# Softmax rows multiplied into W on GpSimd instead of VectorE, with one store per image

## Chip, cores and metric

One core of one Trainium2 chip. The metric is the device time of one execution in microseconds (us). The kernel before takes 877.63 us (median of 3 runs, 877.34 to 877.78).

## What is computed

For each of 32 images x of 384 channels and 1024 pixels (32 x 32), with 12 heads of 32 channels:

```python
w = einsum('bnc,oc->bno', group_norm(x), qkv_w)       # first product, split in 12 heads
w_normed = w / max(sqrt(sum over pixels of w*w), 1e-12)
Pi = softmax over heads of (sum over d of w_normed**2) * temp
Pi_n = Pi / (sum over pixels of Pi + 1e-8)
dots = einsum('bhn,bhnd->bhd', Pi_n, w * w)
attn = 1.0 / (1.0 + dots)
out = -(w * Pi) * attn                                # a row of Pi for each head, a number of attn for each channel
y = x + einsum('bnc,oc->bno', out, out_w) + out_b     # second product
```

All of it is in float32. Each product is computed as three TensorE products of rounded parts: high by high, low by high, high by low.

## The kernel before

Channels lie on the 128 partitions in T = 3 tiles of 128 channels by 1024 pixels (N). A tile of work on VectorE, ScalarE or GpSimd is thus 128x1024. The five engines each run a hand-written program whose order is fixed; semaphores alone tie them together. `pipeline` runs `step(i)` for i = 0 to 32: two steps written out, a loop over 28 images in fours, and the last ones written out. In step i the engines finish image i-2, carry out the second half of image i-1 and the first half of image i.

TensorE, step i: `first_product(i, t)` for t = 0, 1, 2 (W of image i into PSUM `acc`), then `second_product(i-1, t)` for t = 0, 1, 2. Inside the first of these, before its `UL` terms, stand the `head_sums(i)` (line 579), which need the sums of squares of all three tiles of image i, by way of VectorE's `head_sum_weights` (lines 717 to 731). The second product reads `UH` and `UL`, the high and low parts of W weighted by Pi and attn.

ScalarE, step i: `square_w(0)` (line 399, into WS, with the sum of squares), `keep_w(0)` (line 408, W from PSUM into WV), `u_hi(0)` (line 389, UH from WV), `square_w(1)`, `u_hi(1)`, `u_hi(2)`, `square_w(2)`, the two small group-norm activations, `keep_w(1)`, `keep_w(2)`, then `normalise` and `x_hi` for image i+1 (lines 416, 427), with the softmax exponentials between.

VectorE, step i: `finish(i-2, 2)` (line 849, product plus bias plus x, into X), `dot(i-1, t)` three times (line 769: Pi times squares, summed over pixels), the four small operations of `attention(i-1)` (lines 781 to 787), `weigh(i-1, t)` three times (line 795: WV times the scale times Pi, in place), `u_lo` for tiles 0 and 1 (line 841), `group_moments`, `head_sum_weights(i)`, `group_norm`, `u_lo` for tile 2, statistics of image i+2 (line 656), the softmax (lines 738 to 758, which ends with the rows PIT), more statistics, `finish(i-1, 0)` and `finish(i-1, 1)`.

GpSimd, step i: `x_lo(i+1, t)` three times (line 349: XL = XN - XH), nothing else.

SyncE, step i: store tile 2 of image i-2, wait for the stores of that image, load image i+2 (1.5 MB), `spread_pi(i)`: three small writes of PIT to HBM (line 309) and three reads (line 314) that bring the softmax rows back as PIB, spread over 32 partitions each and with 33 numbers for every 32 pixels; then store tiles 0 and 1 of image i-1.

The last image has an order of its own (`last_step`, `attend_last` at line 798): for each tile the dot, four small operations and the weighing (line 812) in turn, so that its UH can start early.

Of the kernel before, what the change touches and what calls it, by code (L numbers as in the profile page):

```python
# [27 lines left out]
ALU = mybir.AluOpType  # L28
ACT = mybir.ActivationFunctionType
# [17 lines left out]
IDLE_TURNS = (6, 3, 1, 15)  # L47
SM_SHIFTED, SM_STEPS = 3, 8
ATTENDED = 3 + 4
U_STEPS = ATTENDED + 3  # L50
LAST_ATTENDED, LAST_WEIGHED = 5, 6


class Image:
# [28 lines left out]
def conv_attention(nc, x, qkv_w, temp, out_w, out_b, y):  # L83
# [15 lines left out]
    with ExitStack() as ctx:  # L99
# [6 lines left out]
        def sem(name):  # L106
            return ctx.enter_context(nc.semaphore(name))
# [91 lines left out]
        pi_written = [sem(f"pi_written_{t}") for t in range(T)]  # L199
        pi_spread = [sem(f"pi_spread_{t}") for t in range(T)]  # L200
        u_step = sem("u_step")
        uh_done = sem("uh_done")
        ul_done = [sem(f"ul_done_{t}") for t in range(T)]
        m2_done = sem("m2_done")
# [14 lines left out]

            return not isinstance(j.number, int) or 0 <= j.number < B  # L220

        def weighed(j, t):

            if has(j) and not has(j + 1):
                return j.counts(U_STEPS, t * LAST_WEIGHED + LAST_WEIGHED)
            return j.counts(U_STEPS, ATTENDED + t + 1)

        def norm_of(j):

# [44 lines left out]
        @block.sync  # L274
        def _(sp):
            def load(j):
                if has(j):
                    if j.follows(2):
                        sp.wait_ge(x_loaded, j.counts(16, -16))
                    sp.dma_start(X[:, j.slot, :], j.of(x_img)).then_inc(x_loaded, 16)  # L280


            for t in range(T):
                sp.dma_start(x_tile(FIRST, t), FIRST.of(x_img)[:, t * N:(t + 1) * N]).then_inc(first_loaded[t], 16)
            sp.dma_start(raw_w1, qkv_w.rearrange("(t p) c -> p t c", t=T)).then_inc(w1_loaded, 16)
            sp.dma_start(raw_w2, out_w.rearrange("(p t) o -> p (t o)", t=T)).then_inc(w2_loaded, 16)
            for j in range(1, SLOTS):
                load(Image(j, j))

            def store(j, t):  # L290
                if has(j):
                    sp.wait_ge(y_done, j.counts(T, t + 1))
                    sp.dma_start(j.of(y_img)[:, t * N:(t + 1) * N], x_tile(j, t)).then_inc(y_stored, 16)

            def store_half(j, t, h):

                sp.wait_ge(y_done, j.counts(T, t + h + 1))
                columns = slice(t * N + h * BANK, t * N + (h + 1) * BANK)
                sp.dma_start(j.of(y_img)[:, columns], X[:, j.slot, columns]).then_inc(y_stored, 16)

            def spread_pi(j):

                if has(j):


                    sp.wait_ge(sm_step, j.counts(SM_STEPS, SM_STEPS))
                    for t in range(T):
                        rows = pi_dram[t * HPT:(t + 1) * HPT].rearrange("h (b q n) -> q (h b) n", b=BLOCKS, q=QUADS)
                        sp.dma_start(rows, PIT[:, t, :]).then_inc(pi_written[t], 16)
                    for t in range(T):  # L310
                        sp.wait_ge(pi_written[t], j.counts(16, 16))
                        heads = pi_dram[t * HPT:(t + 1) * HPT].unsqueeze(0)\
                            .to_broadcast([D, HPT, BLOCKS * QUADS * (QUAD + 1)])
                        sp.dma_start(PIB[:, t].rearrange("p b n -> p (b n)"), heads).then_inc(pi_spread[t], 16)

            def step(i):
                store(i - 2, 2)
                if has(i - 2) and has(i + 2):
                    sp.wait_ge(y_stored, (i - 2).counts(T * 16, T * 16))
                    load(i + 2)  # L320
                spread_pi(i)
                store(i - 1, 0)
                store(i - 1, 1)

            write_stats(sp, FIRST + 1)
            gather_stats(sp, FIRST + 1)
            pipeline(sp, step, 0, B)
            for h in range(HALVES):
                store_half(Image(B - 1, B - 1), T - 1, h)
            sp.wait_ge(y_stored, (B * T + HALVES - 1) * 16)  # L330

        @block.gpsimd
        def _(pool):

            pool.memset(identity[:], 0.0).then_inc(masks_step, 1)
            pool.memset(head_mask[:], 0.0).then_inc(masks_step, 1)
            pool.wait_ge(masks_step, 2)
            pool.affine_select(out=identity[:], in_=identity[:], compare_op=ALU.not_equal, fill=1.0, base=0,
                               pattern=[[-1, P]], channel_multiplier=1).then_inc(masks_step, 1)
            pool.wait_ge(w2_loaded, 16)  # L340
            pool.tensor_copy(mixed_w2.rearrange("p (m d h) -> p m d h", d=D, h=HPT),
                             raw_w2.rearrange("p (m h d) -> p m d h", d=D, h=HPT)).then_inc(w2_mixed, 1)

            def x_lo(j, t):
                if has(j) and j.follows(1):
                    pool.wait_ge(xn_done, j.counts(T, t + 1))
                    pool.wait_ge(xh_done, j.counts(T, t + 1))
                    pool.wait_ge(m1_done, j.counts(T))
                    pool.tensor_tensor(XL[:, t, :], XN[:, t, :], XH[:, t, :].bitcast(F32),  # L349
                                       ALU.subtract).then_inc(xl_done, 1)  # L350

            def step(i):
                for t in range(T):
                    x_lo(i + 1, t)

            pipeline(pool, step, 0, B)

        @block.scalar
        def _(act):
# [21 lines left out]
            def step(i):  # L381
                def u_hi(t):
                    j = i - 1
                    if has(j):
                        act.wait_ge(u_step, weighed(j, t))
                        if j.follows(1):
                            act.wait_ge(m2_done, j.counts(T))
                            act.wait_ge(ul_done[t], j.counts(1))
                        act.activation(UH[:, t, :], w_tile(j, t), ACT.Copy).then_inc(uh_done, 1)  # L389

                def square_w(t):
                    if has(i):
# [223 lines left out]
        def _(dve):  # L616
# [143 lines left out]
            def in_blocks(tile):  # L760
                return tile.rearrange("p (b n) -> p b n", n=QUAD)

            def dot(j, t):

                if has(j):
# [21 lines left out]
                    done = dve.scalar_tensor_tensor(dots[:, 3], total, SUM_FLOOR, inverse, ALU.add, ALU.mult)  # L787
                done.then_inc(u_step, 1)

            def weigh(j, t):  # L790

                if has(j):
                    dve.wait_ge(u_step, j.counts(U_STEPS, ATTENDED))
                    dve.wait_ge(w_kept, j.counts(T, t + 1))
                    dve.scalar_tensor_tensor(in_blocks(w_tile(j, t)), in_blocks(w_tile(j, t)), dots[:, 3, t:t + 1],  # L795
                                             PIB[:, t, :, 0:QUAD], ALU.mult, ALU.mult).then_inc(u_step, 1)

            def attend_last(j, t):

                total, dot_t, both, inverse = pi_tot[:, t:t + 1], dots[:, 0, t:t + 1], dots[:, 1, t:t + 1], dots[:, 2, t:t + 1]  # L800
                base = j.counts(U_STEPS, t * LAST_WEIGHED)
                dot(j, t)
                dve.tensor_reduce(total, PIB[:, t, :, QUAD], AX_X, ALU.add).then_inc(u_step, 1)
                dve.wait_ge(u_step, base + 2)
                dve.scalar_tensor_tensor(both, total, SUM_FLOOR, dot_t, ALU.add, ALU.add).then_inc(u_step, 1)
                dve.wait_ge(u_step, base + 3)
                dve.reciprocal(inverse, both).then_inc(u_step, 1)
                dve.wait_ge(u_step, base + 4)
                dve.scalar_tensor_tensor(dots[:, 3, t:t + 1], total, SUM_FLOOR, inverse, ALU.add, ALU.mult).then_inc(u_step, 1)
                dve.wait_ge(u_step, base + LAST_ATTENDED)  # L810
                dve.wait_ge(w_kept, j.counts(T, t + 1))
                dve.scalar_tensor_tensor(in_blocks(w_tile(j, t)), in_blocks(w_tile(j, t)), dots[:, 3, t:t + 1],  # L812
                                         PIB[:, t, :, 0:QUAD], ALU.mult, ALU.mult).then_inc(u_step, 1)

            def finish_half(j, t, h):

# [17 lines left out]
            def u_lo(j, t):  # L834

                if has(j):
                    dve.wait_ge(uh_done, j.counts(T, t + 1))
                    dve.wait_ge(u_step, weighed(j, t))
                    if j.follows(1):
                        dve.wait_ge(m2_done, j.counts(T))  # L840
                    dve.tensor_tensor(UL[:, t, :], w_tile(j, t), UH[:, t, :].bitcast(F32),  # L841
                                      ALU.subtract).then_inc(ul_done[t], 1)

            def finish(j, t):

# [6 lines left out]
            def step(i):  # L852
# [8 lines left out]
                weigh(i - 1, 0)  # L861
                weigh(i - 1, 1)
                weigh(i - 1, 2)
                u_lo(i - 1, 0)
                u_lo(i - 1, 1)
                group_moments(i + 1)
# [67 lines left out]
```

## Time and profile before

| | |
|---|---|
| median of 3 runs | 877.63 us |
| profiled execution | 877.32 us, span 875.4 us |
| TensorE (matmuls) busy | 855.1 us, 98% |
| VectorE busy | 746.8 us, 85% |
| ScalarE busy | 528.0 us, 60% |
| GpSimd busy | 225.5 us, 26% |
| mean share of the DMA engines, q1 | 51.9% |
| mean granted TensorE clock | 0.995 |

The span runs from the first to the last instruction of the profiled execution. Engines overlap, so the shares don't add up. The profile names PE for TensorE, PEld for its weight loads, DVE for VectorE, ACT for ScalarE, POOL for GpSimd, SP for SyncE; L769 is line 769. A busy share says how much an engine works, not which work the end waits for; that is in the chain of work that ended last.

### The profile page before, as it was taken

The numbers are of one execution on the slowest core, as the hardware profiler recorded it, in microseconds if no ns is written. First come the engines' busy times: TensorE is split into PE (matmuls) and PEld (weight loads), VectorE is DVE, ScalarE is ACT, GpSimd is POOL, SyncE is SP. The second block draws the span as 40 slices with busy tenths as digits, with TensorE's granted clock in tenths as the row PEclk, the third lists the DMA queues.
The fourth block names the chain that finished last, engine by engine and source line by source line (L and its number), as shares of the span: only waits on it lengthen the run. The fifth ranks groups of instructions, "written<-read, shape, count | busy, mean of one in ns | idle before, by whom it ended". The sixth has DMA issues, their size and how long they took to land.

```text
span 875.4 us, 14196 instructions
## 1 busy us (share of the span) xinstructions
PE 855.1 (98%) x4298; PEld 682.2 (78%) x4298; DVE 746.8 (85%) x1377; ACT 528.0 (60%) x676; POOL 225.5 (26%) x101
## 2 busy tenths in 40 slices
PE   6799999999999999999999999999999999999996
PEld 6577787777787777787777787777787777787785
DVE  7598888898888898888889888898888889888767
ACT  3575556676555676555676555677555677555631
POOL 1321233321233331233331133331133331133300
PEclk9899999999999999999999999999999999999999
DMA  7316655446655445665445665545664545664424
GB/s 279 113 42 220 225 167 192 149 178 215 224 185 192 144 176 201 224 198 179 155 170 196 224 204 173 164 171 187 224 218 159 176 160 187 222 224 153 132 74 165
DMA packets 54996, 158.47 MB, mean 181 GB/s; under 512 B 21442, under 2 KB 25794, under 8 KB 51010
## 3 DMA queue, kind: packets, MB, share of 16 engines
q1 hardware_dynamic: 46192, 155.48, 51.9%
q10 hardware_dynamic: 8786, 2.77, 1.3%
q8 instruction: 9, 0.15, 0.1%
q14 instruction: 9, 0.07, 0.0%
HBM read 105.70 MB, written 52.53 MB: 181 GB/s over the span
## 4 chain that ended last, share of the span: by engine, by line
PE 93%; DVE 3%; DMA 2%; issue 1%; ACT 1%; SPq 0%; DVEq 0%; ACTq 0%
PE acc L498 87%; PE scores L579 5%; DMA PIB<-pi 1%; DMA bias<-in_L_conv_out_b 1%; DVE WS L769 1%; DVE stats L656 0%; PE acc L481 0%; DVE XL L714 0%; DVE UL L841 0%; DMA pi<-PIT 0%; DVE WV L812 0%; DVE W2L L630 0%; DVE W1L L630 0%; ACT WV L408 0%; DVE XN L706 0%
## 5 line engine op out<-in xcount | busy, mean ns | idle before, releaser
L349 POOL TENSOR_TENSOR XL<-XN,XH 128x1024 fp32r<-128x1024 f32 x93 | 222.5, 2409 | 589.8 <-ACT XH L427 589.8
L399 ACT ACTIVATE WS<-acc 128x1024 f32<-128x1024 f32 x96 | 97.9, 1020 | 227.4 <-PE acc L498 213.2
L498 PE MATMUL acc<-XH,W1H 128*128 128x512 f32 x576 | 179.1, 392 | 3.9 <-ACT XH L427 3.7
L498 PE MATMUL acc<-UH,W2H 128*128 128x512 f32 x576 | 178.1, 390 | 2.6 <-ACT UH L389 2.5
L498 PE MATMUL acc<-XH,W1L 128*128 128x512 f32 x576 | 178.4, 391 | 0.0
L498 PE MATMUL acc<-UH,W2L 128*128 128x512 f32 x576 | 177.8, 390 | 0.0
L849 DVE SCALAR_TENSOR_TENSOR X<-acc,bias,X 128x1024 f32<-128x1024 f32 x95 | 118.8, 1276 | 38.0 <-PE acc L498 38.0
L498 PE MATMUL acc<-UL,W2H 128*128 128x512 f32 x576 | 149.9, 396 | 0.0
L769 DVE CUSTOM_DVE_ANT_0 WS<-PIB,WS 128x1024 f32<-128x1024 f32 x96 | 117.3, 1223 | 36.5 <-DMA PIB<-pi 35.8
L498 PE MATMUL acc<-XL,W1H 128*128 128x512 f32 x576 | 147.2, 391 | 0.2 <-DVE XL L714 0.2
L389 ACT ACTIVATE UH<-WV 128x1024 fp32r<-128x1024 f32 x96 | 98.1, 1054 | 78.3 <-DVE WV L795 61.2
L498 PEld LDWEIGHTS acc<-UL,W2H 128*128 128x128 f32 x576 | 105.7, 188 | 33.4 <-issue 12.8
L498 PEld LDWEIGHTS acc<-XH,W1H 128*128 128x128 f32 x576 | 108.3, 189 | 28.0 <-issue 2.8
L498 PEld LDWEIGHTS acc<-UH,W2H 128*128 128x128 f32 x576 | 107.9, 188 | 26.3 <-ACT UH L389 3.6
L498 PEld LDWEIGHTS acc<-XL,W1H 128*128 128x128 f32 x576 | 108.8, 189 | 23.2 <-DVE XL L714 0.6
L498 PEld LDWEIGHTS acc<-XH,W1L 128*128 128x128 f32 x576 | 108.7, 189 | 22.8
L498 PEld LDWEIGHTS acc<-UH,W2L 128*128 128x128 f32 x576 | 108.2, 188 | 22.8
L656 DVE BATCH_NORM_STATS2 stats<-X 128x6 f32<-128x512 f32 x192 | 119.7, 679 | 2.5 <-DMA X<-in_x 2.5
L427 ACT ACTIVATE XH<-X,norm 128x1024 fp32r<-128x1024 f32 x96 | 118.1, 1232 | 0.0
L795 DVE SCALAR_TENSOR_TENSOR WV<-WV,dots,PIB 128x1024 f32<-128x1024 f32 x93 | 114.0, 1281 | 1.1
L416 ACT ACTIVATE XN<-X,norm 128x1024 f32<-128x1024 f32 x93 | 114.8, 1235 | 0.0
L841 DVE TENSOR_TENSOR UL<-WV,UH 128x1024 fp32r<-128x1024 f32 x96 | 114.4, 1220 | 0.0
(84 smaller groups left out, 439.9 us busy)
## 6 DMA issues: line engine op xcount, KB each, us to landing
PIB<-pi SPq DMA_DIRECT2D x96, 528.0 KB, 6.1
out_y<-X SPq DMA_DIRECT2D x95, 512.0 KB, 7.4
X<-in_x SPq DMA_DIRECT2D x31, 1536.0 KB, 6.3
gathered<-stats_rows ACTq DMA_DIRECT2D x30, 72.0 KB, 6.7
pi<-PIT SPq DMA_DIRECT2D x96, 16.5 KB
X<-in_x SPq DMA_DIRECT2D x3, 512.0 KB, 4.6
WV<-in_L_conv_qkv_w SPq DMA_DIRECT2D x1, 576.0 KB, 6.7
WS<-in_L_conv_out_w SPq DMA_DIRECT2D x1, 576.0 KB, 7.6
```

What stands on the lines that cost most here:

```text
L349: pool.tensor_tensor(XL[:, t, :], XN[:, t, :], XH[:, t, :].bitcast(F32), ALU.subtract).then_inc(xl_done, 1)
L389: act.activation(UH[:, t, :], w_tile(j, t), ACT.Copy).then_inc(uh_done, 1)
L399: act.activation(square_tile(i, t), acc[:, t, :], ACT.Square, accum_out=sumsq[:, t:t + 1]).then_inc(squared, 1)
L416: act.activation(XN[:, t, :], x_tile(j, t), ACT.Identity, bias=shift_j, scale=rstd_j).then_inc(xn_done, 1)
L427: act.activation(XH[:, t, :], x_tile(j, t), ACT.Identity, bias=shift_j, scale=rstd_j).then_inc(xh_done, 1)
L498: last = pe.matmul(out[:, h * BANK:(h + 1) * BANK], w[:, k, m * P:(m + 1) * P], r[:, k, h * BANK:(h + 1) * BANK], start=(n == 0 and k == 0 ...
L579: last = pe.matmul(scores[q * QUAD:(q + 1) * QUAD, 0:N // QUADS], headsum[:, t, :], block_q, start=(t == 0), stop=(t == T - 1))
L656: last = dve.bn_stats(stats[:, t * HALVES + h, :], x_tile(j, t)[:, h * BANK:(h + 1) * BANK])
L769: dve.tensor_tensor_reduce(in_blocks(square_tile(j, t)), PIB[:, t, :, 0:QUAD], in_blocks(square_tile(j, t)), 1.0, 0.0, ALU.mult, ALU.add, ...
L795: dve.scalar_tensor_tensor(in_blocks(w_tile(j, t)), in_blocks(w_tile(j, t)), dots[:, 3, t:t + 1], PIB[:, t, :, 0:QUAD], ALU.mult, ALU.mult ...
L841: dve.tensor_tensor(UL[:, t, :], w_tile(j, t), UH[:, t, :].bitcast(F32), ALU.subtract).then_inc(ul_done[t], 1)
L849: dve.scalar_tensor_tensor(x_tile(j, t), acc[:, t, :], bias[:, t:t + 1], x_tile(j, t), ALU.add, ALU.add).then_inc(y_done, 1)
```

## The change

GpSimd gets `value(j, t)`: WV = WV * PIB, in place, for each tile of each image, once the tile is kept and its rows have landed. VectorE's `weigh` goes (and the weighing in `attend_last`). The per-channel scale, `dots[:, 3]`, is applied later, by both users: `u_hi` takes it as the scale of its activation, and `u_lo` becomes a `scalar_tensor_tensor`, WV * scale - UH. Both now wait for the scale and for GpSimd's product. The rows may be overwritten by the next image's only once GpSimd has read them. And each image but the last is stored by one DMA of 1.5 MB after its last tile; the last image is stored in four parts as before.

```diff
-            def store(j, t):
+            def store(j):
                 if has(j):
-                    sp.wait_ge(y_done, j.counts(T, t + 1))
-                    sp.dma_start(j.of(y_img)[:, t * N:(t + 1) * N], x_tile(j, t)).then_inc(y_stored, 16)
+                    sp.wait_ge(y_done, j.counts(T, T))
+                    sp.dma_start(j.of(y_img), X[:, j.slot, :]).then_inc(y_stored, 16)
...
             def spread_pi(j):
...
+                    if j.follows(1):
+                        sp.wait_ge(value_done, j.counts(T))
                     sp.wait_ge(sm_step, j.counts(SM_STEPS, SM_STEPS))
...
             def step(i):
-                store(i - 2, 2)
+                store(i - 2)
                 if has(i - 2) and has(i + 2):
-                    sp.wait_ge(y_stored, (i - 2).counts(T * 16, T * 16))
+                    sp.wait_ge(y_stored, (i - 2).counts(16, 16))
                     load(i + 2)
                 spread_pi(i)
-                store(i - 1, 0)
-                store(i - 1, 1)
...
+            def value(j, t):
+
+                if has(j):
+                    pool.wait_ge(w_kept, j.counts(T, t + 1))
+                    pool.wait_ge(pi_spread[t], j.counts(16, 16))
+                    pool.tensor_tensor(in_blocks(w_tile(j, t)), in_blocks(w_tile(j, t)), PIB[:, t, :, 0:QUAD],
+                                       ALU.mult).then_inc(value_done, 1)
...
             def step(i):
                 for t in range(T):
                     x_lo(i + 1, t)
+                for t in range(T):
+                    value(i, t)
...
                     if has(j):
-                        act.wait_ge(u_step, weighed(j, t))
+                        wait_scale(act, j, t)
+                        act.wait_ge(value_done, j.counts(T, t + 1))
...
-                        act.activation(UH[:, t, :], w_tile(j, t), ACT.Copy).then_inc(uh_done, 1)
+                        act.activation(UH[:, t, :], w_tile(j, t), ACT.Copy, scale=scale_of(t)).then_inc(uh_done, 1)
...
-            def weigh(j, t):
-
-                if has(j):
-                    dve.wait_ge(u_step, j.counts(U_STEPS, ATTENDED))
-                    dve.wait_ge(w_kept, j.counts(T, t + 1))
-                    dve.scalar_tensor_tensor(in_blocks(w_tile(j, t)), in_blocks(w_tile(j, t)), dots[:, 3, t:t + 1],
-                                             PIB[:, t, :, 0:QUAD], ALU.mult, ALU.mult).then_inc(u_step, 1)
...
                 if has(j):
+                    wait_scale(dve, j, t)
+                    dve.wait_ge(value_done, j.counts(T, t + 1))
                     dve.wait_ge(uh_done, j.counts(T, t + 1))
-                    dve.wait_ge(u_step, weighed(j, t))
                     if j.follows(1):
                         dve.wait_ge(m2_done, j.counts(T))
-                    dve.tensor_tensor(UL[:, t, :], w_tile(j, t), UH[:, t, :].bitcast(F32),
-                                      ALU.subtract).then_inc(ul_done[t], 1)
+                    dve.scalar_tensor_tensor(UL[:, t, :], w_tile(j, t), scale_of(t), UH[:, t, :].bitcast(F32), ALU.mult,
+                                             ALU.subtract).then_inc(ul_done[t], 1)
```

## Rows read from the trace of the kernel before

**Rows 1.** The page's part 4, shares of the chain by engine.

```profile
PE 93%; DVE 3%; DMA 2%; issue 1%; ACT 1%; SPq 0%; DVEq 0%; ACTq 0%
```

**Rows 2.** TensorE by windows: stretch, length, busy (instructions), clock, DMA share, GB/s.

```profile
60.00:840.00 780.00, 779.88 (x3924) 1.00 0.55 185
```

**Rows 3.** The chain in order of time (start, us, what): `head_sums` of images 1 and 31.

```profile
55.81 1.50 PE scores L579 x24
...
840.68 1.43 PE scores L579 x24
```

**Rows 4.** The page's part 5: line, engine, shapes, count | busy, mean ns | idle before.

```profile
L349 POOL TENSOR_TENSOR XL<-XN,XH 128x1024 fp32r<-128x1024 f32 x93 | 222.5, 2409 | 589.8 <-ACT XH L427 589.8
...
L849 DVE SCALAR_TENSOR_TENSOR X<-acc,bias,X 128x1024 f32<-128x1024 f32 x95 | 118.8, 1276 | 38.0 <-PE acc L498 38.0
...
L769 DVE CUSTOM_DVE_ANT_0 WS<-PIB,WS 128x1024 f32<-128x1024 f32 x96 | 117.3, 1223 | 36.5 <-DMA PIB<-pi 35.8
...
L389 ACT ACTIVATE UH<-WV 128x1024 fp32r<-128x1024 f32 x96 | 98.1, 1054 | 78.3 <-DVE WV L795 61.2
...
L795 DVE SCALAR_TENSOR_TENSOR WV<-WV,dots,PIB 128x1024 f32<-128x1024 f32 x93 | 114.0, 1281 | 1.1
L416 ACT ACTIVATE XN<-X,norm 128x1024 f32<-128x1024 f32 x93 | 114.8, 1235 | 0.0
L841 DVE TENSOR_TENSOR UL<-WV,UH 128x1024 fp32r<-128x1024 f32 x96 | 114.4, 1220 | 0.0
```

**Rows 5.** Timeline of VectorE in one steady step: start us, us, instruction, [idle before].

```profile
408.50 1.22 DVE L769 CUSTOM_DVE_ANT_0 WS<-PIB,WS 128x1024 f32<-128x1024 f32 x1
...
413.17 0.33 DVE L781 TENSOR_REDUCE pi_tot<-PIB 128x3 f32<-128x96 f32 x1
...
413.94 0.16 DVE L787 SCALAR_TENSOR_TENSOR dots<-pi_tot,dots 128x3 f32<-128x3 f32 x1
...
421.26 0.26 DVE L729 TENSOR_TENSOR headsum<-head_temp,inv 128x96 f32<-128x96 f32 x1
...
427.34 0.26 DVE L758 TENSOR_REDUCE PIT<-PIT 128x3 f32<-128x96 f32 x1
```

**Rows 6.** Timeline of ScalarE in the same step.

```profile
415.46 1.06 ACT L389 ACTIVATE UH<-WV 128x1024 fp32r<-128x1024 f32 x1 [1.89 <-DVE WV L795]
...
419.70 1.03 ACT L399 ACTIVATE WS<-acc 128x1024 f32<-128x1024 f32 x1 [0.28 <-PE acc L498]
```

**Rows 7.** Timeline of GpSimd, its last two `x_lo` before that step's dots.

```profile
402.51 4.76 POOL L349 TENSOR_TENSOR XL<-XN,XH 128x1024 fp32r<-128x1024 f32 x2 [0.53 <-ACT XH L427]
```

**Rows 8.** Timeline of TensorE: start of `second_product`, and the head sums.

```profile
419.34 0.62 PE L498 MATMUL acc<-UH,W2H 128*128 128x512 f32 x2
...
422.15 1.50 PE L579 MATMUL scores<-WS,headsum 128*32 128x256 f32 x24
```

**Rows 9.** Timeline of SyncE's queue: spreading the rows, loading image i+2.

```profile
403.92 1.85 SPq L314 DMA_DIRECT2D PIB<-pi  x3
...
416.22 0.35 SPq L280 DMA_DIRECT2D X<-in_x  x1
...
429.79 1.85 SPq L314 DMA_DIRECT2D PIB<-pi  x3
```

**Rows 10.** Tile PIB from 380 to 440 us: time from issue to landing.

```profile
DMA to landing us min/median/max: 4.0/6.2/6.9
```

**Rows 11.** Timeline of VectorE, first image: its first dot and the end of `attention`.

```profile
43.34 1.23 DVE L769 CUSTOM_DVE_ANT_0 WS<-PIB,WS 128x1024 f32<-128x1024 f32 x1 [4.14 <-DMA PIB<-pi]
...
48.31 0.16 DVE L787 SCALAR_TENSOR_TENSOR dots<-pi_tot,dots 128x3 f32<-128x3 f32 x1
```

**Rows 12.** Timeline of the last image: first dot, last UH, TensorE's UL terms.

```profile
853.11 1.22 DVE L769 CUSTOM_DVE_ANT_0 WS<-PIB,WS 128x1024 f32<-128x1024 f32 x1
...
862.73 1.06 ACT L389 ACTIVATE UH<-WV 128x1024 fp32r<-128x1024 f32 x1 [2.11 <-DVE WV L812]
...
866.74 4.24 PE L498 MATMUL acc<-UL,W2H 128*128 128x512 f32 x18
```

More of the change, by code:

```diff
@@ L49 @@
 ATTENDED = 3 + 4
-U_STEPS = ATTENDED + 3
-LAST_ATTENDED, LAST_WEIGHED = 5, 6
+U_STEPS = ATTENDED
+TILE_STEPS = 4
 class Image:
@@ L201, in conv_attention @@
         u_step = sem("u_step")
+        tile_step = sem("tile_step")
+        value_done = sem("value_done")
         uh_done = sem("uh_done")
@@ L220, in has, with by_tiles, scale_of, wait_scale @@
             return not isinstance(j.number, int) or 0 <= j.number < B
[L222 to L226, printed above, removed]
+        def by_tiles(j):
+            return has(j) and not has(j + 1)
+        def scale_of(t):
+            return dots[:, 3, t:t + 1]
+        def wait_scale(eng, j, t):
+            if by_tiles(j):
+                eng.wait_ge(tile_step, TILE_STEPS * (t + 1))
+            else:
+                eng.wait_ge(u_step, j.counts(U_STEPS, ATTENDED))
+        def in_blocks(tile):
+            return tile.rearrange("p (b n) -> p b n", n=QUAD)
         def norm_of(j):
@@ L288, in _, with store_part @@
                 load(Image(j, j))
-            def store(j, t):
+            def store(j):
                 if has(j):
-                    sp.wait_ge(y_done, j.counts(T, t + 1))
-                    sp.dma_start(j.of(y_img)[:, t * N:(t + 1) * N], x_tile(j, t)).then_inc(y_stored, 16)
-            def store_half(j, t, h):
-                sp.wait_ge(y_done, j.counts(T, t + h + 1))
-                columns = slice(t * N + h * BANK, t * N + (h + 1) * BANK)
+                    sp.wait_ge(y_done, j.counts(T, T))
+                    sp.dma_start(j.of(y_img), X[:, j.slot, :]).then_inc(y_stored, 16)
+            def store_part(j, begin, end, finished):
+                sp.wait_ge(y_done, j.counts(T, finished))
+                columns = slice(begin, end)
                 sp.dma_start(j.of(y_img)[:, columns], X[:, j.slot, columns]).then_inc(y_stored, 16)
@@ L327, in _ @@
             pipeline(sp, step, 0, B)
+            last = Image(B - 1, B - 1)
+            for t in range(T - 1):
+                store_part(last, t * N, (t + 1) * N, t + 1)
             for h in range(HALVES):
-                store_half(Image(B - 1, B - 1), T - 1, h)
-            sp.wait_ge(y_stored, (B * T + HALVES - 1) * 16)
+                store_part(last, (T - 1) * N + h * BANK, (T - 1) * N + (h + 1) * BANK, T + h)
+            sp.wait_ge(y_stored, (B - 1 + T - 1 + HALVES) * 16)
         @block.gpsimd
@@ L758, in softmax_divide @@
                 link(dve.tensor_reduce(PIT[:, :, QUAD], PIT[:, :, 0:QUAD], AX_X, ALU.add), follows=False)
-            def in_blocks(tile):
-                return tile.rearrange("p (b n) -> p b n", n=QUAD)
             def dot(j, t):
@@ L788, in attention @@
                 done.then_inc(u_step, 1)
-            def weigh(j, t):
-                if has(j):
-                    dve.wait_ge(u_step, j.counts(U_STEPS, ATTENDED))
-                    dve.wait_ge(w_kept, j.counts(T, t + 1))
-                    dve.scalar_tensor_tensor(in_blocks(w_tile(j, t)), in_blocks(w_tile(j, t)), dots[:, 3, t:t + 1],
-                                             PIB[:, t, :, 0:QUAD], ALU.mult, ALU.mult).then_inc(u_step, 1)
             def attend_last(j, t):
                 total, dot_t, both, inverse = pi_tot[:, t:t + 1], dots[:, 0, t:t + 1], dots[:, 1, t:t + 1], dots[:, 2, t:t + 1]
-                base = j.counts(U_STEPS, t * LAST_WEIGHED)
+                base = TILE_STEPS * t
                 dot(j, t)
[L803 to L813, printed above, removed]
+                dve.tensor_reduce(total, PIB[:, t, :, QUAD], AX_X, ALU.add).then_inc(tile_step, 1)
+                dve.wait_ge(tile_step, base + 1)
+                dve.wait_ge(u_step, j.counts(U_STEPS, t + 1))
+                dve.scalar_tensor_tensor(both, total, SUM_FLOOR, dot_t, ALU.add, ALU.add).then_inc(tile_step, 1)
+                dve.wait_ge(tile_step, base + 2)
+                dve.reciprocal(inverse, both).then_inc(tile_step, 1)
+                dve.wait_ge(tile_step, base + 3)
+                dve.scalar_tensor_tensor(scale_of(t), total, SUM_FLOOR, inverse, ALU.add, ALU.mult).then_inc(tile_step, 1)
             def finish_half(j, t, h):
@@ L860, in step @@
                     attention(i - 1, k)
-                weigh(i - 1, 0)
-                weigh(i - 1, 1)
-                weigh(i - 1, 2)
                 u_lo(i - 1, 0)
```

## Prediction

> **What bounds the kernel now.** First the chain of work that ended last: 93% of it is TensorE [rows 1]. Then TensorE by windows: from 60 to 840 us it is busy for 779.88 of 780 us at full clock [rows 2]. So in the middle only something that makes TensorE wait can change the time; work taken off VectorE gains nothing there by itself. The period is (840.68 - 55.81) / 30 = 26.16 us an image, from one `head_sums` to the next [rows 3]. What is left is the start (until 55.81) and the end (34.7 us from the last head sums to 875.4).
>
> Next the timelines of one steady step, to see how much room the loop behind TensorE has. It is a loop because the head sums of image i+1 need the sums of squares, which ScalarE makes after `u_hi` of image i, which waits for `attention` of image i, which waits for the dots, the spread rows, the softmax, and so for the head sums of image i. I follow it once, each leg as short as its own work allows:
> - A, from the end of `attention` to `headsum` ready: from the first UH to the last square 419.70 - 415.46 = 4.24 us, less the 0.28 us that it waited for TensorE, is 3.96 [rows 6]; from the last square to the end of L729 421.52 - 419.70 = 1.82 [rows 5, 6]; with 0.05 for the hand-over 5.8 us.
> - B, from `headsum` ready (421.52) to PIT done (427.60): 6.1 us [rows 5]. VectorE is packed here.
> - C, from PIT done to the first tile of PIB landed: reads issued at 429.79, 2.2 us later [rows 9], the first lands 4.0 us after its issue at the least [rows 10] and 4.6 at the most, since the dot at 408.50 didn't wait for a read issued at 403.92 [rows 5, 9]; with 4.3, 6.5 us.
> - D, from there to the end of `attention`: dots and four small operations. Three dots of 1.16 to 1.23 us [rows 4, 5] and 414.10 - 413.17 = 0.93 us [rows 5] are 4.5 us if nothing holds them.
> That is 22.9 us of 26.16. Seen at `attention`: it ends at 414.10, and could end 2.1 us later, because 414.10 + 5.8 = 419.9 against head sums that start at 422.15 [rows 5, 8].
>
> **Removed.** Three weighings of 1.28 us an image on VectorE [rows 4], and with them the wait of ScalarE's first UH for the first one (415.46 against 414.10). In the steady step that is cover that TensorE doesn't need: 0 us. In the first image the head sums start at 55.81; from the end of `attention` (48.47) [rows 11] plus A, 5.8, they could start at 54.3, but TensorE's own terms end at about 55.1 (the head sums follow the start of the second product by 2.8 us when nothing waits [rows 8], and it starts at 52.2): -0.7 us. At the end three weighings stand in a row before the last UH (862.73) [rows 12]; the last UH could start 3 x 1.2 = 3.6 us earlier, but the first one only 1.2, and TensorE then has its own 36 matmuls to run (18 take 4.24 us [rows 12]). So between -1.2 and -3.6, I take -2.2 us.
>
> **Added on GpSimd.** Three products of two SBUF tiles. `x_lo` is the same operation and shape without the gaps of PIB: 2.41 us [rows 4]; 7.2 us an image. GpSimd is free from 407.27 [rows 7] until the next XH, which ScalarE makes after its last square at 419.70 [rows 6]. PIB's first tile lands at about 408.2, so GpSimd by itself is done at 415.4, or at 418.7 with 3.5 us for each. The last UH has to start by 420.1 to be there for TensorE's third pair of terms at 421.15. So even a product 45% dearer than `x_lo` is hidden, if GpSimd and VectorE don't hold each other up.
>
> **Do they?** That is the whole question. The products begin at 408.2, and at 408.50 VectorE begins its dots, each of which reads two SBUF tiles (WS and PIB). In the trace GpSimd always works beside VectorE operations with at most one tile in SBUF (statistics, and `finish`, whose `acc` is in PSUM): both keep their durations. Its work ends at 407.27 [rows 7], before the dots at 408.50; no row shows it beside a dot, a UL or a weighing. So the cost has two bounds. Side by side: D stays 4.5 us. One after the other: D is 3 x 2.41 + 3 x 1.2 + 0.93 = 11.8 us. Which? A dot with two SBUF tiles takes 1.22 us, no more than `finish` with one [rows 4], so VectorE reads both streams at once; GpSimd takes twice that for the same count. Two engines would then ask for three or four streams together, where the rows never show more than GpSimd's and one of VectorE's. I take the one-after-the-other end, since the overlap that rows show undisturbed is exactly the one without a second SBUF stream of VectorE.
>
> Of this the Trainium skill, page "SBUF — State Buffer", section "Who interferes with whom", says: a VectorE instruction with two SBUF inputs contends with a GpSimd instruction that reads SBUF, and the one that starts first keeps the shared port for its whole length while the other blocks. By it D is the serial sum; a kernel in which it didn't hold would keep its period. No run here shows it yet.
>
> GpSimd starts 0.3 us before VectorE, so the first dot waits. Whatever the order after that, the sum up to `attention` is nearly the same, because the small operations L783 and L787 read two SBUF operands too and queue behind a running product. The loop is then A + B + C + D = 5.8 + 6.1 + 6.5 + 11.8 = 30.2 us instead of 26.16: +4.0 us an image.
>
> **Moved and exchanged.** UH gets a scale from a tile: 0 to 0.18 us each (L416, with pointers, takes 1235 ns, L389 1054 [rows 4]); in a loop that is the bound, up to 0.5 us an image. UL as `scalar_tensor_tensor` costs 1.28 for 1.22 us [rows 4], off the chain. The wait of SyncE for `value_done` precedes a wait for the softmax that ends some 8 us later: nothing is queued behind it that was not before. The single store of 1.5 MB is issued when tile 2 is finished, at 408.5, with the rows of PIB already on their way; the three stores used to end at 416.2, when the load follows [rows 9]. The same bytes; between 0.8 us earlier and about 1 us later, and the load has about 1 us to spare before the statistics: 0. The reads of PIB lose the two stores that ran beside them, 0 to 0.8 us on the second and third tile.
>
> **The sum.** First image: its first dot starts at 43.34 and `attention` ends at 48.47 [rows 11]. With D = 11.8 it ends at 55.1, `headsum` is ready 5.8 us later, and the head sums start at 61.0: +5.2 us. Then 30 periods of 30.2 instead of 26.16: +121 us. At the end the first dot starts at 853.1 [rows 12]; GpSimd can begin earlier, as soon as the rows land, and I give it most of one product ahead (1.7 us). The rest is 3 x 2.41 - 1.7 + 3 x 1.2 = 9.1 us in turn and the last small operations about 0.9, so the last scale is there at 863.1 against a last UH at 862.73 [rows 12]: +0.4. Sum +126.6 us: span 1002, and with the 1.9 us around the span (877.32 - 875.4) 1003.9; the median lies 0.3 us above the profiled run: **1004 us**. The ScalarE term and a gappy product of up to 2.6 us (3 x 0.2) add up to 1.1 us an image: 1038. Overlap of fixed parts and a few fewer waits take up to 0.7 us an image: 983.
>
> **Rivals.**
> - *No hindrance* (faster): GpSimd's products and the dots run side by side. Place: 408 to 416 in each step; it decides as long as `attention` ends before 416.2. Then the period stays and start and end gain 0.7 + 2.2: 874.7 us. For it: GpSimd beside `finish` costs neither anything. Against: that is one SBUF stream of VectorE. Chance 0.17.
> - *VectorE gets its turn first* after the first product, with all three dots (408.2 + 2.4 + 3.6 + 0.9 = 415.1, within the slack of 2.1 us). Then the two late products and the first UL share the time, the last product ends at about 420.1, the last square at 422.2 and the head sums at 423.0: +0.85 us x 31 = 26, 904 us. Sharing at a finer grain, with each slowed by half, ends between: up to 980. Chance 0.15.
> - *The product over PIB's gaps is much dearer* than `x_lo`, 3.5 us, and serial: 3 x 1.1 x 31 = +100 us on top, 1100. For it nothing but that no row has this access; chance 0.03.
> - *The store holds up the load*, and the statistics with it: at most 1 us x 28 on a kernel that is otherwise as fast as now, 900 us. Chance 0.02. A change without effect, gains and losses cancelling within 0.2%: 0.02.
>
> **Chances.** One after the other, 983 to 1038: 0.61. VectorE first or sharing 0.15, dearer product 0.03, store 0.02: slower by over 0.2% has 0.81, faster 0.17, within 0.2% 0.02. 0.2% (1.8 us) is about what a measurement of this kernel can tell from no change. The range reaches from 890, which takes in the VectorE-first case, to 1040; left out are the fast cases (0.19).
>
> **What would show it.** The group L769: mean well over 1.22 us, or idle before it ended by GpSimd; GpSimd's new group starting about 0.3 us before the first dot of a step; idle of TensorE before UH or before the head sums of 4 us a period; head sums 30.2 us apart. Dots of 1.22 us with products beside them and head sums 26.16 us apart would make the forecast wrong, and a period of 27 us would say that VectorE goes first.

## The result, and the profile after

The changed kernel takes 968.6 us (median of 4 runs, 967.7 to 970.0) against 877.5 us in the same job: ratio 1.104 (95% interval 1.103 to 1.106). It is slower by 91 us, where 126 were forecast. Its profiled execution has a span of 967.2 us against 875.4, 91.8 us more, and this is the difference that I take apart.

The page of the changed kernel, parts 1 and 4 (busy time and share by engine; shares of the chain that ended last) and the groups of part 5 that answer to [rows 1, 4]:

```profile
PE 881.7 (91%) x4298; PEld 676.3 (70%) x4298; DVE 811.3 (84%) x1281; ACT 534.9 (55%) x676; POOL 511.7 (53%) x197
...
PE 45%; DVE 20%; issue 14%; DMA 9%; ACT 8%; SPq 1%; ACTq 1%; DVEq 1%
...
L375 POOL TENSOR_TENSOR XL<-XN,XH 128x1024 fp32r<-128x1024 f32 x93 | 222.5, 2408 | 384.4 <-ACT XH L456 384.3
L367 POOL TENSOR_TENSOR WV<-WV,PIB 128x1024 f32<-128x1024 f32 x96 | 286.2, 3009 | 41.3 <-DMA PIB<-pi 41.3
L795 DVE CUSTOM_DVE_ANT_0 WS<-PIB,WS 128x1024 f32<-128x1024 f32 x96 | 260.8, 2750 | 12.3 <-DMA PIB<-pi 11.8
L527 PE MATMUL acc<-UH,W2H 128*128 128x512 f32 x576 | 190.1, 412 | 48.8 <-ACT UH L418 48.7
...
L418 ACT ACTIVATE UH<-WV,dots 128x1024 fp32r<-128x1024 f32 x96 | 106.7, 1142 | 180.9 <-DVE dots L813 163.9
```

TensorE's share of the chain has gone from 93% to 45%. VectorE lost 96 weighings of 1.28 us, 123 us, and is busy for 64 us more than before: the same 96 dots take 2750 ns on average, not 1223. An engine that waits inside an instruction is shown as busy. TensorE now idles 48.7 us before `UH`, and ScalarE's UH waits 163.9 us for the end of `attention` (L813).

The timeline of one steady step of the changed kernel, VectorE, GpSimd and ScalarE; it answers to [rows 5 to 7]:

```profile
465.44 0.26 DVE L758 TENSOR_TENSOR headsum<-head_temp,inv 128x96 f32<-128x96 f32 x1
...
471.76 0.26 DVE L787 TENSOR_REDUCE PIT<-PIT 128x3 f32<-128x96 f32 x1
...
478.40 3.26 DVE L795 CUSTOM_DVE_ANT_0 WS<-PIB,WS 128x1024 f32<-128x1024 f32 x1
...
481.58 3.22 DVE L795 CUSTOM_DVE_ANT_0 WS<-PIB,WS 128x1024 f32<-128x1024 f32 x1
...
484.74 3.22 DVE L795 CUSTOM_DVE_ANT_0 WS<-PIB,WS 128x1024 f32<-128x1024 f32 x1
...
488.65 0.16 DVE L813 SCALAR_TENSOR_TENSOR dots<-pi_tot,dots 128x3 f32<-128x3 f32 x1
...
478.37 8.50 POOL L367 TENSOR_TENSOR WV<-WV,PIB 128x1024 f32<-128x1024 f32 x3 [0.58 <-DMA PIB<-pi]
...
488.85 1.15 ACT L418 ACTIVATE UH<-WV,dots 128x1024 fp32r<-128x1024 f32 x1 [5.38 <-DVE dots L813]
```

GpSimd starts 0.03 us before the first dot, and each dot takes 3.16 us from start to start instead of 1.16. Read from the trace image by image, this is the order in 16 of the 31 images before the last. In the other 15 the two start within 0.11 us of each other, the first dot goes first and is not held (1.22 us); the product takes its turn after it, and the wait comes out at the small operation L809 instead. One such step, VectorE and GpSimd:

```profile
129.38 1.22 DVE L795 CUSTOM_DVE_ANT_0 WS<-PIB,WS 128x1024 f32<-128x1024 f32 x1
...
131.01 2.73 DVE L795 CUSTOM_DVE_ANT_0 WS<-PIB,WS 128x1024 f32<-128x1024 f32 x1 [0.40 <-DMA PIB<-pi]
...
137.17 1.79 DVE L809 SCALAR_TENSOR_TENSOR dots<-pi_tot,dots 128x3 f32<-128x3 f32 x1
...
129.43 9.52 POOL L367 TENSOR_TENSOR WV<-WV,PIB 128x1024 f32<-128x1024 f32 x3 [0.70 <-DMA PIB<-pi]
```

From the first of the two to start until the end of `attention` it takes 10.4 us in the first order and 10.0 us in the second. The first and the last head sums, for [rows 3]:

```profile
58.80 1.50 PE L608 MATMUL scores<-WS,headsum 128*32 128x256 f32 x24 [0.56 <-DVE headsum L758]
...
928.75 1.50 PE L608 MATMUL scores<-WS,headsum 128*32 128x256 f32 x24 [0.55 <-DVE headsum L758]
```

So the 91.8 us lie as follows: 58.80 - 55.81 = 3.0 at the start; (928.75 - 58.80) / 30 = 29.00 us an image instead of 26.16, which is 85.2; and 967.2 - 928.75 = 38.5 instead of 34.8 from the last head sums to the end, 3.7.

### The profile page after: what moved, and what is told of

Its sections match the earlier page's. It is cut to its first block, busy times and chain, and to the rows that moved or that the text cites. A ratio compares the mean times of both kernels' runs of the same rounds, so it can differ in the third digit from the quotient of the medians.

```text
span 967.2 us, 14056 instructions
## 1 busy us (share of the span) xinstructions
PE 881.7 (91%) x4298; PEld 676.3 (70%) x4298; DVE 811.3 (84%) x1281; ACT 534.9 (55%) x676; POOL 511.7 (53%) x197
## 4 chain that ended last, share of the span: by engine, by line
PE 45%; DVE 20%; issue 14%; DMA 9%; ACT 8%; SPq 1%; ACTq 1%; DVEq 1%
PE acc L527 42%; DVE WS L795 9%; DMA PIB<-pi 6%; ACT UH L418 4%; PE scores L608 3%; ACT WS L428 3%; DMA pi<-PIT 2%; DVE stats L685 2%; DVE dots L809 1%; DVE group_mv L712 1%; SPq L326 1%; DVE headsum L758 1%; DVE UL L857 1%; DMA bias<-in_L_conv_out_b 1%; SPq L331 0%
## 5 line engine op out<-in xcount | busy, mean ns | idle before, releaser
L367 POOL TENSOR_TENSOR WV<-WV,PIB 128x1024 f32<-128x1024 f32 x96 | 286.2, 3009 | 41.3 <-DMA PIB<-pi 41.3
L795 DVE CUSTOM_DVE_ANT_0 WS<-PIB,WS 128x1024 f32<-128x1024 f32 x96 | 260.8, 2750 | 12.3 <-DMA PIB<-pi 11.8
L527 PE MATMUL acc<-UH,W2H 128*128 128x512 f32 x576 | 190.1, 412 | 48.8 <-ACT UH L418 48.7
L418 ACT ACTIVATE UH<-WV,dots 128x1024 fp32r<-128x1024 f32 x96 | 106.7, 1142 | 180.9 <-DVE dots L813 163.9
L527 PE MATMUL acc<-UH,W2L 128*128 128x512 f32 x576 | 180.9, 396 | 0.0
L857 DVE SCALAR_TENSOR_TENSOR UL<-WV,dots,UH 128x1024 fp32r<-128x1024 f32 x96 | 123.1, 1284 | 67.7 <-ACT UH L418 67.7
L527 PEld LDWEIGHTS acc<-UH,W2H 128*128 128x128 f32 x576 | 102.5, 190 | 99.1 <-ACT UH L418 60.1
L527 PEld LDWEIGHTS acc<-XH,W1H 128*128 128x128 f32 x576 | 108.1, 189 | 29.1 <-ACT XH L456 3.5
```

The source lines that it names most:

```text
L367: pool.tensor_tensor(in_blocks(w_tile(j, t)), in_blocks(w_tile(j, t)), PIB[:, t, :, 0:QUAD], ALU.mult).then_inc(value_done, 1)
L418: act.activation(UH[:, t, :], w_tile(j, t), ACT.Copy, scale=scale_of(t)).then_inc(uh_done, 1)
L527: last = pe.matmul(out[:, h * BANK:(h + 1) * BANK], w[:, k, m * P:(m + 1) * P], r[:, k, h * BANK:(h + 1) * BANK], start=(n == 0 and k == 0 ...
L795: dve.tensor_tensor_reduce(in_blocks(square_tile(j, t)), PIB[:, t, :, 0:QUAD], in_blocks(square_tile(j, t)), 1.0, 0.0, ALU.mult, ALU.add, ...
L857: dve.scalar_tensor_tensor(UL[:, t, :], w_tile(j, t), scale_of(t), UH[:, t, :].bitcast(F32), ALU.mult, ALU.subtract).then_inc(ul_done[t], 1)
```

## The experiments

**Theory A**: a VectorE instruction that reads two operands in SBUF and a GpSimd instruction that reads SBUF take turns, whole instruction by whole instruction. **Theory B**: GpSimd's product is slow by itself over PIB's gaps (its mean is 3009 ns), and the new waits carry that to TensorE. The other parts of the change, store and scale, had to be cleared as well.

**One stream less on VectorE.** The changed kernel, where the dots of all images but the last take their second operand from PSUM (the squares are left out of them):

```diff
-                    dve.tensor_tensor_reduce(in_blocks(square_tile(j, t)), PIB[:, t, :, 0:QUAD],
-                                             in_blocks(square_tile(j, t)), 1.0, 0.0,
+                    other = in_blocks(square_tile(j, t))
+                    if not by_tiles(j):
+                        other = small[:, 0:QUAD].unsqueeze(1).to_broadcast([P, BLOCKS * QUADS, QUAD])
+                    dve.tensor_tensor_reduce(in_blocks(square_tile(j, t)), PIB[:, t, :, 0:QUAD], other, 1.0, 0.0,
```

> The changed kernel, but for all images except the last the dot takes its second operand from a PSUM tile instead of WS (the sum of squares is left out of the dots, so attn is not the real one). Same instructions, same waits, same products on GpSimd; VectorE's dots now read one SBUF tile instead of two. Theory A (a VectorE instruction with two SBUF inputs and a GpSimd instruction that reads SBUF take turns): dots go back to 1.2 to 1.3 us beside the products, products to the 2.15 us that is their shortest in the changed kernel; the two-input small operation after them may still wait up to 2 us, which the slack of 2.1 us covers; head sums 26.2 us apart, 880 us (start +1, end +3.8 kept, since the last image is unchanged). Theory B (GpSimd's product is simply slow over PIB's gaps, 3.2 us, or the new waits cost the time): products stay at 3.2 us, the period stays near 29.0 and the time near 968 us.

Measured 881.2 us, ratio to before 1.004 (1.002 to 1.007); head sums (840.65 - 56.07) / 30 = 26.15 us apart. VectorE and GpSimd in one step:

```profile
460.85 1.21 DVE L798 CUSTOM_DVE_ANT_1 WS<-PIB,small 128x1024 f32<-128x1024 f32 x1
...
463.13 1.22 DVE L798 CUSTOM_DVE_ANT_1 WS<-PIB,small 128x1024 f32<-128x1024 f32 x1
...
464.65 0.20 DVE L811 SCALAR_TENSOR_TENSOR dots<-pi_tot,dots 128x3 f32<-128x3 f32 x1
...
465.10 1.91 DVE L815 SCALAR_TENSOR_TENSOR dots<-pi_tot,dots 128x3 f32<-128x3 f32 x1
...
460.47 6.52 POOL L367 TENSOR_TENSOR WV<-WV,PIB 128x1024 f32<-128x1024 f32 x3 [0.83 <-DMA PIB<-pi]
```

The dots run beside the products and neither notices: 1.22 us and 2.17 us each. All that is left is one small operation of three columns, which does read two SBUF operands and waits for the third product: here L815, 1.91 us instead of 0.16, and in most images L811 (median 1.75 us). The loop's slack of 2.1 us covers it. The last image is as in the changed kernel, and its end costs the 4 us by which this run is above the kernel before. This run alone decides between A and B: waits, products and gaps are those of the changed kernel, and the whole 85 us are gone. It also rules out a tile read by both engines as the cause: these dots still read PIB beside the products, while the small operation that waits shares no tile with them.

**Products after the dots.** The changed kernel with

```diff
                     pool.wait_ge(pi_spread[t], j.counts(16, 16))
+                    if not by_tiles(j):
+                        pool.wait_ge(u_step, j.counts(U_STEPS, T))
```

> The changed kernel, but GpSimd's products of every image but the last also wait for the third dot, so they can't run beside a dot. Theory A: dots 1.22 us; products 2.15 us, beginning after the third dot; the two-input small operations of attention (L809, L813) now meet the products and wait about 2 us each; attention ends 8.9 us after the first rows land instead of 10.4, period about 27.5 us, 923 us. Theory B (products slow by themselves, 3.2 us each): they end 9.5 us after the third dot, the last UH comes 4 us later than now, period 30 us or more, over 995 us.

Measured 924.8 us (1.054; 1.051 to 1.058), head sums (884.42 - 58.03) / 30 = 27.55 us apart.

```profile
459.45 1.23 DVE L797 CUSTOM_DVE_ANT_0 WS<-PIB,WS 128x1024 f32<-128x1024 f32 x1
...
460.97 2.02 DVE L811 SCALAR_TENSOR_TENSOR dots<-pi_tot,dots 128x3 f32<-128x3 f32 x1
463.02 0.18 DVE L813 RECIPROCAL dots<-dots 128x3 f32<-128x3 f32 x1
463.23 1.91 DVE L815 SCALAR_TENSOR_TENSOR dots<-pi_tot,dots 128x3 f32<-128x3 f32 x1
...
460.77 6.51 POOL L369 TENSOR_TENSOR WV<-WV,PIB 128x1024 f32<-128x1024 f32 x3 [4.77 <-DVE dots L797]
```

Starting the products later makes the kernel 44 us faster than the change, which B excludes. The two operations with two SBUF operands pay 1.86 and 1.75 us for 0.16 us of work; the reciprocal between them, with one, pays nothing. The first UL, which reads WV and UH, meets the end of the third product: 1.82 us for 1.28.

**Products after attention.** The same line with `ATTENDED` for `T`.

> The changed kernel, but the products of all images except the last wait for the end of attention, so they meet neither a dot nor a small operation; what they can still meet is UL of tile 0 and 1, which reads WV and UH. Theory A: dots 1.22 us, L809 and L813 0.16 us; the products end one by one 2.2, 4.4 and 6.6 us after attention, so now the UH themselves wait for products, and the third product or the first UL waits for the other (0 to 1.2 us more); head sums 27.1 to 28.1 us apart, 912 to 943 us. UL of tile 0 is lengthened by up to 1 us. If UL doesn't contend, 27.1 us and UL stays at 1.28 us.

Measured 952.2 us (1.085; 1.082 to 1.089), head sums (911.80 - 58.87) / 30 = 28.43 us apart, more than the expected 27.1 to 28.1.

```profile
450.31 1.80 DVE L859 SCALAR_TENSOR_TENSOR UL<-WV,dots,UH 128x1024 fp32r<-128x1024 f32 x1 [3.73 <-ACT UH L420]
452.48 2.78 DVE L859 SCALAR_TENSOR_TENSOR UL<-WV,dots,UH 128x1024 fp32r<-128x1024 f32 x1 [0.37 <-ACT UH L420]
...
454.26 1.15 ACT L420 ACTIVATE UH<-WV,dots 128x1024 fp32r<-128x1024 f32 x1 [1.99 <-POOL WV L369]
...
446.67 7.51 POOL L369 TENSOR_TENSOR WV<-WV,PIB 128x1024 f32<-128x1024 f32 x3 [6.12 <-DVE dots L815]
```

I had counted on one UL meeting a product. Both do: 1.80 and 2.78 us for 1.28, and the third product ends at 454.2, 0.9 us late, with the last UH behind it. In all three places that were tried between the landing of PIB and the last UH (beside the dots, after them, after `attention`) the products met two-stream work of VectorE.

**Products twice.** The changed kernel with each product made twice, so that W is weighted by Pi twice.

> The changed kernel with each product done twice (the second multiplies by PIB again, so the output is not the reference's). Theory A with turns taken per instruction: 3 x 2.15 = 6.5 us more GpSimd work an image, all of it in series with VectorE's two-input work until attention has ended; a dot still waits for one product only, so attention ends between 0 and 1 us later, and what is late is the third product itself, which ends 6.5 us later; period 29.0 + 4 to 5.5 = 33 to 34.5 us, 1090 to 1140 us. If instead both engines are slowed in proportion while the other works (sharing at a fine grain), the dots stay at 3.2 us only as long as they need, and products beyond the dots take 2.15 us too; the time is then the same, but the dots' lengths would not be pinned to the products' ends. Read: do dot ends coincide with product ends.

Measured 1084.6 us (1.237; 1.233 to 1.240), head sums (1042.83 - 63.26) / 30 = 32.65 us apart, a little under the expected 33 to 34.5. Not all of that is waiting: TensorE's granted clock is 0.92 between 60 and 1000 us, against 1.00 in the changed kernel, since it falls to the lower level after the longer idle in the steps. So this run is not read by its time. Here GpSimd's instructions stand singly, so the turns can be read (VectorE, then GpSimd):

```profile
470.30 3.21 DVE L799 CUSTOM_DVE_ANT_0 WS<-PIB,WS 128x1024 f32<-128x1024 f32 x1
...
473.44 3.21 DVE L799 CUSTOM_DVE_ANT_0 WS<-PIB,WS 128x1024 f32<-128x1024 f32 x1
...
469.36 3.06 POOL L371 TENSOR_TENSOR WV<-WV,PIB 128x1024 f32<-128x1024 f32 x1
472.38 3.18 POOL L368 TENSOR_TENSOR WV<-WV,PIB 128x1024 f32<-128x1024 f32 x1
475.64 3.06 POOL L371 TENSOR_TENSOR WV<-WV,PIB 128x1024 f32<-128x1024 f32 x1
478.66 2.18 POOL L368 TENSOR_TENSOR WV<-WV,PIB 128x1024 f32<-128x1024 f32 x1
```

The product ends at 472.42, and the dot that was waiting gives way to the next one at 473.44, 1.02 us later; the next product ends at 475.56, 2.12 us after that; the next dot at 476.58, again 1.02. (By its own record, which overlaps the next, a dot ends 0.07 us later.) Each engine's record holds its own work and the other's turn: 1.0 + 2.15 = 3.15. The last product shown, with no dot beside it, takes 2.18. Two slowed engines without turns would give neither these ends nor that sum.

**GpSimd writes and doesn't read.** The products are replaced by memsets of the same tiles, with a one-column operation in front that carries the waits (W is lost).

> The changed kernel with each product replaced by a memset of the same tile (and a one-column operation in front of it that carries the waits), so GpSimd writes a 128x1024 tile and reads practically nothing; W is lost, the output is not the reference's. Theory A, turns only where GpSimd reads: dots 1.22 us even beside the memsets; period 26.2 us, 875 to 880 us. Rival: any GpSimd access of SBUF blocks VectorE: each dot is lengthened by a memset of about 1 us, attention ends 2 to 3 us later than in the kernel before, period 26.2 to 27 us, up to 905 us.

Measured 873.7 us (0.996; 0.995 to 0.998), head sums (839.87 - 55.27) / 30 = 26.15 us apart.

```profile
460.07 1.22 DVE L799 CUSTOM_DVE_ANT_0 WS<-PIB,WS 128x1024 f32<-128x1024 f32 x1
...
462.36 1.22 DVE L799 CUSTOM_DVE_ANT_0 WS<-PIB,WS 128x1024 f32<-128x1024 f32 x1
...
459.77 0.95 POOL L372 MEMSET WV<- 128x1024 f32 x1
...
462.41 1.23 POOL L371 TENSOR_TENSOR pool_cell<-ones 128x1 f32<-128x1 f32 x1 [0.18 <-DMA PIB<-pi]
```

Writing the whole tile beside a dot costs nothing. Reading one column does: the one-column operation takes 0.20 us alone and 1.23 us when it comes 0.05 us after a dot, since it waits for the dot to end. No run has a GpSimd operation with a single input beside the dots: both of these read two.

**The rest of the change.** Three runs say what isn't to blame. First the changed kernel with the products on VectorE:

```diff
+            def value(j, t):
+
+                if has(j):
+                    dve.wait_ge(w_kept, j.counts(T, t + 1))
+                    dve.tensor_tensor(in_blocks(w_tile(j, t)), in_blocks(w_tile(j, t)), PIB[:, t, :, 0:QUAD],
+                                      ALU.mult).then_inc(value_done, 1)
...
                     attention(i - 1, k)
+                for t in range(T):
+                    value(i - 1, t)
```

> The changed kernel with only the engine of the products undone: VectorE multiplies WV by PIB after attention (and after each small chain of the last image); one store per image, the scale in UH and UL and all waits stay. If only the place of the products costs time: 877.5 us, within 0.2% of the kernel before (UH 0.1 us longer is hidden; the products take 1.22 instead of 1.28 us). If the store or the scale is part of the loss: over 880 us.

Measured 876.9 us, ratio 0.9993 (0.9984 to 1.0002): store, scale and the added waits together cost nothing that can be seen. Then the kernel before with the stores of the change alone:

> The kernel before with the stores of the change alone: one of 1.5 MB per image but the last. Loads start within 1 us of where they start now, statistics have about 1 us to spare: 877.5 us, within 0.2%. If the single store delays the loads beyond that: up to 28 us more.

Measured 876.7 us, 0.9994 (0.9985 to 1.0003). And the changed kernel with the last image's products on VectorE:

> The changed kernel with the last image's three products on VectorE, as before the change. The end of the changed kernel (38.5 us from the last head sums, against 34.7 before) is then 34.7 again: 968.6 - 3.8 = 964.8 us, if the blocked small operations and the clock at half level after TensorE's idle of 5 us are what the end costs. If the end is long for another reason (stores): 968 us.

Measured 965.8 us (1.101; 1.099 to 1.102): 2.8 us less than the change. In its trace 965.1 - 929.65 = 35.4 us follow the last head sums, so the end is cured of 3.0 of its 3.7 us, while the period stays at 28.97. (The kernel with all products on VectorE has the same 35.4 us there.) Its first images are those of the changed kernel, and yet its head sums of image 1 start at 60.51 instead of 58.80: a difference of this size at the start needs no cause in the kernel.

**How long is a product?**

> e1_psum_dot with one thing more: GpSimd's product writes its tile as fp32r (rounded) instead of f32, in the same place. It asks why a product takes 2.2 us where x_lo, which also reads two tiles, takes 2.41: if the rounded output costs it, products go to 2.4 us; if the subtraction or the gaps of PIB make the difference, they stay at 2.2. No effect on the period either way: about 881 us.

Measured 881.0 us in a single run; the two groups of GpSimd:

```profile
L375 POOL TENSOR_TENSOR XL<-XN,XH 128x1024 fp32r<-128x1024 f32 x93 | 222.6, 2408 | 371.4 <-ACT XH L456 371.3
L367 POOL TENSOR_TENSOR WV<-WV,PIB 128x1024 fp32r<-128x1024 f32 x96 | 209.7, 2212 | 42.7 <-DMA PIB<-pi 42.7
```

It is not the output type. Whether multiplying is quicker than subtracting, or two inputs of this shape are, stays open.

**A version that beats both.** Products on VectorE as above, except that of tile 0 of the last image, which GpSimd makes:

> As e2 (products on VectorE), but the product of tile 0 of the last image is GpSimd's. In the kernel before GpSimd and then VectorE idle there until finish; the rows land about 1.5 us before the dot can start. Theory A: it holds up the first dot by up to 0.5 us and saves a 1.2 us multiplication before the first UH, and shortens the chain to the last UH by the same 0.7 us: 876.5 to 877.2 us, 0.05 to 0.1% faster than before. If GpSimd's product were slow by itself (3.2 us): no gain.

Measured 875.1 us, ratio to before 0.9972 (0.9961 to 0.9983): 0.28% faster, more than expected, and 1.9 us under the 876.9 us with all products on VectorE. The end in its trace:

```profile
850.57 2.19 POOL L375 TENSOR_TENSOR WV<-WV,PIB 128x1024 f32<-128x1024 f32 x1 [26.58 <-DMA PIB<-pi]
...
852.31 1.53 DVE L803 CUSTOM_DVE_ANT_0 WS<-PIB,WS 128x1024 f32<-128x1024 f32 x1
...
854.59 1.15 ACT L426 ACTIVATE UH<-WV,dots 128x1024 fp32r<-128x1024 f32 x1 [11.88 <-DVE dots L843]
```

The product lies mostly beside `finish`, which has one SBUF tile, and costs the dot 0.3 us (1.53). The first UH starts 2.3 us after the dot instead of 3.3, and 33.6 us follow the last head sums instead of 34.8. The head sums of image 1 start at 55.22 instead of 55.81, but that has nothing to do with this product: they start at 55.31 in the run with the stores alone and at 55.16 with all products on VectorE.

The right partner for a comparison is therefore the latter, the same kernel but for this product. There 35.4 us follow the last head sums, so all of the 1.9 us lie at the end. They come in two halves. TensorE's first matmul stands 16.0 us behind the last head sums instead of 16.9, and its 36 matmuls from there to the UL terms take 864.79 - 855.79 = 9.0 us instead of 866.50 - 856.62 = 9.9: there the first 3.4 us ran at a granted clock of 0.54, here none did. The second half is not owed to the earlier UH for certain, since the clock at this place differs between executions of the same work (last section).

## Why the prediction was right, and where its sizes were off

The direction, the place and the kind of wait were right; the size was not as good as the range makes it look. 968.6 us lies below the 983 to 1038 us that the forecast gave to turns one after the other, and inside the 904 to 980 us of its second rival (VectorE first, or sharing at a finer grain). By the time alone one would have picked that rival. The rows say otherwise: in 15 of 31 images VectorE does start first, but after one dot a product takes its turn, not after three, and the dots' ends are tied to the products' ends. It is only because the stated range reached down to 890 for the sake of the rival that it holds the result.

**What bounds the kernel, and the slack**: right. With work off VectorE and no turns (memsets) the period stays 26.15. The slack of 2.1 us held a delay of 1.75 us in the run with one stream less.

**Do they hinder each other?** Right: D is a serial sum. The forecast named the place and the sign. That GpSimd is ahead holds in 16 images of 31 (by 0.03 us in the step shown, by up to 0.6 us elsewhere); that the order hardly changes the sum held: 10.4 and 10.0 us. The rule of the Trainium skill, page "SBUF — State Buffer", section "Who interferes with whom", which stood beside it, agrees with the runs: two SBUF inputs against a GpSimd read take turns (3.15 us a pair), one input (dots of 1.22 us) and a GpSimd write (memsets of 0.95 us) don't. Only its "whole length" is a little more than was measured: 1.0 of a dot's 1.22 us.

**The size of D** is the term that was off. Forecast 11.8 us; measured 488.81 - 478.37 = 10.4 us. Two entries were too large: the product, priced by `x_lo` at 2.41, takes 2.15 to 2.2; and of a dot's 1.2 us only 1.0 stands in line with the product. A pair is 3.15, not 3.6, three pairs 9.5, and with 0.93 for the small operations 10.4. The forecast had allowed for this kind of error, but with 0.7 us an image instead of the 1.2 that came. The other legs, read in the step shown: A 465.70 - 459.72 = 6.0 (5.8 forecast), B 472.02 - 465.70 = 6.3 (6.1), C 478.37 - 472.02 = 6.35 (6.5). The sum is 29.1 and the period 29.00, where 30.2 was forecast: 1.2 us times 30 is 36 us too much. With 2.2 us too much at the start and 3.3 too little at the end that makes the 35 us by which the whole forecast was too high. That the small operations queue behind a product is so in the images where a dot starts first: L809 has a mean of 948 ns over the 31 images, 1.8 us in 15 of them and 0.16 in the others.

**The start**: forecast +5.2, measured +3.0. D took 52.7 - 42.7 = 10.0 us instead of 11.8, and the first dot stood at 42.72 instead of 43.34; 0.4 us of that are already there in the head sums of image 0 (31.10 against 31.51), on which the change has no bearing.

**The end**: forecast +0.4, measured +3.7. This step failed. It followed the last UH, and that one did come as late as before: 950.90 - 941.25 = 9.65 us after the first dot, 9.62 before. But the first UH came 947.12 - 941.25 = 5.9 us after that dot instead of 3.3, because two small operations waited 1.9 us each. TensorE has 36 matmuls to run from the first UH on. It idled 4.96 us before them, began them 7.07 us after the first dot instead of 4.39, and took 10.2 us for them instead of 9.2, because it then had a granted clock at the lower of its two levels, 1.2 GHz: 2.7 + 1.0 are the 3.7 us. (In the memset run, at the full clock and without a wait between them, they take 863.90 - 855.54 = 8.4 us.) TensorE in three stretches of the changed kernel's end (length, busy and count, granted clock, DMA share, GB/s):

```profile
928.00:948.30 20.30, 14.81 (x97) 0.94 0.44 160
948.30:952.00 3.70, 3.68 (x9) 0.50 0.02 4
952.00:967.20 15.20, 10.78 (x47) 0.95 0.26 103
```

The forecast of the gain had used just this fact ("the first one only 1.2") and the forecast of the loss had not.

**Removed work is worth nothing in the middle, 0.7 us at the start, 2.2 at the end**: right in the middle and at the end. The memset run, in which nothing holds VectorE up, keeps the period of 26.15 us and ends 32.6 us after the last head sums (-2.2). Its span of 872.5 us and the 1.9 us around it are within 0.4 us of the 874.7 of the rival without hindrance. But that is in part luck: its head sums start at 55.27 (-0.5), and those of the run with the stores alone, which still has all the weighings, start at 55.31. So no run shows that removed work gains anything at the start.

**Scale, UL and store at 0**: right within 0.2%. The scale costs UH 0.09 us (1142 against 1054 ns), half of the upper bound.

## What to carry over

Before work goes from VectorE to GpSimd, list what VectorE will execute meanwhile and count its SBUF inputs: in all these runs an instruction with two of them and a GpSimd instruction that reads SBUF stood in one queue, however small either was. Add them up as a serial sum in the loop that stands behind the busy engine, and compare with its slack. An engine that is free by its busy share may have its free time exactly where its partner does two-stream work; here the one place that brought a gain was beside `finish`, just before the last image's dots.

## Not expected

- A VectorE operation on three columns took about 1.8 to 2.0 us instead of 0.16 behind a GpSimd product, and a GpSimd operation on one column 1.23 us instead of 0.20 behind a dot: the wait goes by the other's instruction, not by one's own size.
- Of a dot of 1.22 us only 1.0 us excludes GpSimd.
- GpSimd multiplies two 128x1024 tiles, one with gaps, in 2.15 to 2.2 us, and subtracts two dense ones in 2.41.
- TensorE's granted clock was 0.50 after an idle of 4.96 us at the end. Idles of nearly one length had different sequels there: with the products on VectorE it was 0.54 for 3.4 us after an idle of 2.24 us; in the kernel before it stayed full after one of 2.27. The run with the stores alone has that same last image, idled 2.28 us, and fell to 0.52 for 3.5 us, from 1.6 us after the idle on; 35.5 us followed its last head sums instead of 34.8. So 0.7 us at the end can differ between two traces without any difference in the last image's work.
